# Last tap of v's convolution: ScalarE and an accumulating transfer in place of a VectorE operation

## The reference, cut to what matters

```python
q = _silu(x @ Wq); k = _silu(x @ Wk); v = _silu(x @ Wv); z = x @ Wz
q = _causal_dwconv(q, conv_q_w)      # depthwise, 4 taps: y[t] = sum_i w[i] * u[t - 3 + i]
k = _causal_dwconv(k, conv_k_w)
v = _causal_dwconv(v, conv_v_w)
...                                  # rotary embedding and normalization of q and k
for s in range(4):
    k_s, v_s, a_s = _lag(k, s), _lag(v, s), _lag(a, s)
    attn = einsum('bshd,bshd->bsh', q, k_s) * scale
    out = out + (attn * sigmoid(a_s * b))[..., None] * v_s
out = out * rsqrt(mean(out * out) + eps) * norm_w * _silu(z)
return out @ Wout
```

## Time and profile before

| | us |
|---|---|
| median of 3 runs | 1383.82 |
| fastest and slowest run | 1382.62, 1384.70 |
| profiled execution | 1383.09 |
| its span, first to last instruction | 1381.0 |
| TensorE busy | 1350.4 |
| VectorE busy | 988.1 |
| ScalarE busy | 737.9 |
| GpSimd busy | 333.3 |

### The profile page before, as it was taken

How to read it: one execution, slowest core, us unless ns; L and a number is a source line. 1 busy time by engine, 2 the same in 40 slices (tenths; PEclk the granted TensorE clock), 3 DMA queues, 4 the chain that set the end, 5 groups by cost and what they waited for, 6 DMA issues and landing times. The chain is left out here.

```text
span 1381.0 us, 23144 instructions
## 1 busy us (share of the span) xinstructions
PE 1350.4 (98%) x6824; PEld 1140.7 (83%) x6824; DVE 988.1 (72%) x1529; ACT 737.9 (53%) x2209; POOL 333.3 (24%) x508
## 2 busy tenths in 40 slices
PE   6999999999999999999999999996999999999998
PEld 4788888888888888888888888885888888888886
DVE  7898998989999999999998999983122222234443
ACT  5656665656656666666566665652654434432221
POOL 6134242323333232323333332422000000000001
PEclk9999999999999999999999999997999999999999
DMA  8233434334344344343433434333421101156454
GB/s 287 62 87 86 101 78 115 93 85 97 95 93 100 85 104 102 80 100 83 108 93 85 100 85 108 78 75 74 152 96 50 46 23 47 36 186 188 129 174 157
DMA packets 123418, 138.79 MB, mean 101 GB/s; under 512 B 30704, under 2 KB 67568, under 8 KB 123120
## 3 DMA queue, kind: packets, MB, share of 16 engines
q1 hardware_dynamic: 114160, 121.48, 31.1%
q0 software_dynamic: 9216, 16.78, 7.1%
HBM read 62.58 MB, written 25.30 MB: 64 GB/s over the span
## 5 line engine op out<-in xcount | busy, mean ns | idle before, releaser
L1169 DVE TENSOR_TENSOR hid_lo<-relu,hid_hi 128x512 fp32r<-128x512 f32 x64 | 44.3, 693 | 172.8 <-ACT hid_hi L1115 172.8
L670 DVE SCALAR_TENSOR_TENSOR y_v<-u_v,cw_v,y_v 128x512 f32<-128x512 f32 x192 | 144.8, 754 | 29.0 <-ACT y_v L561 24.3
L670 DVE SCALAR_TENSOR_TENSOR y_k<-u_k,cw_k,y_k 128x512 f32<-128x512 f32 x192 | 145.2, 756 | 26.1 <-ACT y_k L561 19.2
L581 ACT ACTIVATE bank<-bank 128x128 f32<-128x128 f32 x512 | 133.8, 261 | 46.7 <-PE bank L866 46.4
L670 DVE SCALAR_TENSOR_TENSOR y_q<-u_q,cw_q,y_q 128x512 f32<-128x512 f32 x192 | 144.1, 750 | 19.4 <-ACT y_q L561 10.5
L472 POOL TENSOR_TENSOR rq_win<-rq_win,const 128x32 f32<-128x32 f32 x64 | 21.4, 335 | 478.4 <-DMA rq_win<-rq_scratch 478.4
L1210 DVE TENSOR_TENSOR hid_lo<-o_raw,hid_hi 128x512 fp32r<-128x512 f32 x64 | 44.3, 692 | 101.4 <-ACT hid_hi L1135 101.4
L459 POOL TENSOR_TENSOR rnorm<-norms,neg_half 128x8 f32<-128x8 f32 x64 | 108.4, 1693 | 9.9 <-POOL norms L455 8.9
L1111 ACT ACTIVATE relu<-bank,us_sb 128x512 f32<-128x512 f32 x64 | 44.1, 689 | 121.9 <-PE bank L1250 121.9
L1135 ACT ACTIVATE hid_hi<-o_raw 128x512 fp32r<-128x512 f32 x64 | 40.4, 632 | 121.9 <-PE bank L1280 119.2
L1087 POOL TENSOR_TENSOR g_buf<-g_buf,up_raw 128x512 f32<-128x512 f32 x3 | 3.8, 1281 | 403.2 <-DVE g_buf L1190 403.2
(11 more groups left out here) (170 smaller groups left out, 3455.5 us busy)
## 6 DMA issues: line engine op xcount, KB each, us to landing
swapped_q<-y_q SPq DMA_DIRECT2D x128, 128.0 KB, 2.3
swapped_k<-y_k SPq DMA_DIRECT2D x128, 128.0 KB, 2.3
sq_sum<-out_sq POOLq DMA_DIRECT2D x64, 256.0 KB, 3.3
o_scratch<-o_buf SPq DMA_DIRECT2D x64, 256.0 KB, 2.6
o_raw<-o_scratch SPq DMA_DIRECT2D x64, 256.0 KB, 3.2
raw_q<-in_wq SPq DMA_DIRECT2D x16, 256.0 KB, 3.1
raw_k<-in_wk SPq DMA_DIRECT2D x16, 256.0 KB, 3.5
raw_v<-in_wv SPq DMA_DIRECT2D x16, 256.0 KB, 4.4
```

The source lines that it names most:

```text
L581: last = nc.scalar.activation(block_of, block_of, ACT.Square, accum_out=norms[:, g1 % 2, i * BC + b:i * BC + b + 1])
L670: nc.vector.scalar_tensor_tensor(y[n][:, g % 2, :], u[n][:, g % 2, i:i + CH], cw[n][:, bass.ds(h * TAPS + i, 1)], y[n][:, g % 2, :], ALU.m ...
L1169: nc.vector.tensor_tensor(hid_lo[:, j % 2, :], relu[:, j % 2, :], hid_hi[:, j % 2, :].bitcast(fp32), ALU.subtract).then_inc(hid_lo_done, 1)
```

## The change

The last tap of v (i = 3) is no longer an operation of VectorE. ScalarE makes the product as a scaled copy of `u["v"]` into a buffer of its own, `last_tap`, right behind the first tap. GpSimd's queue adds it to `y["v"]` by an accumulating DMA of 256 KB. GpSimd issues it at the beginning of the next step, ahead of the norms, once ScalarE's copy and VectorE's two remaining taps are done. `turn_v` waits for the landing of this DMA in place of VectorE's third tap. `last_tap` takes the place of `down_raw[:, 1]`, so the second group of FFN weights is loaded in the FFN part and no longer in the prologue.

```diff
+        DVE_TAPS = {"q": 3, "k": 3, "v": 2}
         sq_asked = sem("sq_asked", ctx)
+        last_tap_made = sem("last_tap_made", ctx)
+        last_tap_asked = sem("last_tap_asked", ctx)
+        last_tap_added = sem("last_tap_added", ctx)
+        last_tap = down_raw[:, 1, :, :]
...
-            for i in range(2):
-                env["load_ffn_weights"](sp, i)
+            env["load_ffn_weights"](sp, 0)
             sp.wait_ge(cleared, 6)
...
+            def add_last_tap(g1, c):
+                wait(pool, last_tap_made, c)
+                wait(pool, conv_done["v"], 2 * c)
+                pool.sem_inc(last_tap_asked, 1)
+                nc.gpsimd.dma_start(y["v"][:, g1 % 2, :], last_tap[:, g1 % 2, :], accum_op=ALU.add
+                                    ).then_inc(last_tap_added, 16)
+
             def step(h, g):
                 c = h * G + g
+                if back(h, g, 1):
+                    add_last_tap(back(h, g, 1)[1], c)
                 if at := back(h, g, 1):
...
                 if n == "v":
+                    wait(act, last_tap_added, 16 * (c - 1))
                     wait(act, turned_v, c - 1)
...
+                if n == "v":
+                    nc.scalar.activation(last_tap[:, g % 2, :], u["v"][:, g % 2, HALO:], ACT.Copy,
+                                         scale=cw["v"][:, bass.ds(h * TAPS + HALO, 1)]
+                                         ).then_inc(last_tap_made, 1)
...
                     conv_tap("v", 2, h, g, c)
-                    conv_tap("v", 3, h, g, c)
...
             def turn_v(g1, c):
                 wait(pe, norms_done, c)
-                wait(pe, conv_done["v"], 3 * c)
+                wait(pe, last_tap_added, 16 * c)
...
-            for i in range(2, FT // WG):
+            for i in range(1, FT // WG):
                 wait(sp, up_signed, i - 1)
                 wait(sp, down_signed, i - 1)
                 load_ffn_weights(sp, i)
```

More of the change, by code:

```diff
@@ L544, in silu_and_tap @@
                 wait(act, proj_done[n], c + 1)
-                wait(act, conv_done[n], 3 * (c - 1))
+                wait(act, conv_done[n], DVE_TAPS[n] * (c - 1))
                 nc.scalar.activation(u[n][:, g % 2, HALO:], bank[:, :], ACT.Silu).then_inc(silu_done[n], 1)
-                wait(act, conv_done[n], 3 * c)
+                wait(act, conv_done[n], DVE_TAPS[n] * c)
                 wait(act, silu_done[n], 2 * c + 1)
                 if n == "v":
+                    wait(act, last_tap_added, 16 * (c - 1))
                     wait(act, turned_v, c - 1)
@@ L668, in conv_tap @@
                 else:
-                    wait(dve, conv_done[n], 3 * c + i - 1)
+                    wait(dve, conv_done[n], DVE_TAPS[n] * c + i - 1)
                 nc.vector.scalar_tensor_tensor(
```

## The result

The changed kernel takes 1416.44 us (median of 4 runs, 1414.1 to 1418.87) where the kernel before took 1384.26 beside it. The ratio is 1.0234, with an interval of 1.0214 to 1.0255. That is 32 us slower; the forecast was 26, and its range went up to 1428 us. The profiled execution took 1417.08 us, its span 1415.3 against 1381.0 before.

A forecast was written before the change was run, and what follows sets the result against it. The prediction took attention to be bound by TensorE. Steady steps 14, first late step 2.5, start 5.4, clock 2.5 and end 1.7 summed to 26.1 us on 1383.1, giving 1409 us; own range 1402 to 1422, 8-in-10 range 1393 to 1428.

The forecast's parts named there:

- VectorE and ScalarE cost and give nothing: Attention: 49 us taken from VectorE gain 0; ScalarE's added 0.72 us copy a step costs 0, at most 11 us.
- The need of a steady step: Steady attention steps: time needed from sq_sum's issue to `turn_v`, between 4.5 and 5.8 us, taken as 5.6.
- On average half of d is paid: Steady steps: `turn_v` late by d (0.4 typically, mean 0.8 at g=1) pays half on average, 14 us over 56 steps.
- rival 1: Steady steps hide the transfer, need 4.5 to 5.0; 11 to 14 us lost, 1396 us; chance 0.30.
- How often a g = 1 step is late: Second step of a head: room before `turn_v` 5.0 us in 8 of 13 heads, 4.4 in 5.
- The start: Second `turn_v`: its transfer stands behind `gate_k`, which waits for VectorE's gates; 5.4 us of stall (4.7 to 6.3).
- The clock's 2.0 for 2.5: Behind the start's stall: TensorE's clock may fall to half speed, costing 2.5 us (0 to 3.8).
- The first late step: Head 1, still unrolled: sq_sum only 2.17 us ahead of `turn_v`; 2.5 us of stall (1.6 to 3.4).
- The end: End of attention: last `turn_v` 3.3 to 3.9 us late, half absorbed by a later idle; 1.7 us (0.5 to 2.5).
- SP's loads: Second group of FFN weights moved from prologue to FFN's start: hidden by about 2 us, cost 0.
- Rival 2: Steady steps: second accumulating transfer starts its 3.3 us only once the first has landed; need 6.8, 1446 us; chance 0.12.
- Rival 3: Attention: VectorE did bound, so up to 49 us come back, less the start's 8; down to 1342 us; chance 0.05.

The follow-up runs named there:

- experiment 1: The kernel before without v's last tap on VectorE and nothing in its place: 1383.75 us, ratio 0.9997.
- experiment 2: The kernel before with ScalarE's copy and GpSimd's transfer added, into a buffer nobody reads, VectorE's tap kept: 1382.16 us, ratio 0.9985.
- experiment 5: The changed kernel with an operation of the tap's size on VectorE where the tap was, on data nobody reads: 1418.68 us, ratio 1.0251.
- experiment 4: The changed kernel with `gate_k` of chunk 0 moved behind the last tap's transfer of chunk 1: 1405.58 us, ratio 1.0171.
- experiment 9: The kernel before with only the second group of FFN weights moved to the FFN's start: 1383.94 us, ratio 0.9998.
- experiment 8: The changed kernel with VectorE's two products with sin written as scalar_tensor_tensor by 1.0: 1415.31 us, ratio 1.0235.

## Why the prediction was right, and where its sizes were off

**VectorE and ScalarE cost and give nothing.** Right (experiments 1 and 2). The 0.77 us back to SP in g = 1 steps are nearly right too: against the kernel before the two kinds of room grow by 0.71 and 0.74, and between experiment 5 and the changed kernel by 0.64 to 0.68.

**The need of a steady step.** Its two ends were 4.5 and 5.8, and the value taken, 5.6, is right for a step in which the store overlaps: 5.66. The way there was not quite the forecast's: the second issue begins 0.69 us after the first, not 0.95, and the landing takes 4.9, not 4.65 (5.6 less 0.95). The hint of the rows that the DMA engines are full held: in line behind sq_sum the landing is 4.2 (0.8 more than alone), and with the store 4.9 (0.7 more). By the figures of the Trainium skill (DMA: Bandwidth & Descriptors, Anatomy of one DMA) a landing after 2.6 us is the estimate for 256 KB. The traces disagree: no accumulating transfer of this queue in any run landed in under 3.3.

**The failed step: "On average half of d is paid", with d = 0.4 in a typical step.** The forecast took one need, 5.6, for all steps, because it let the store's bytes start 0.8 us after their issue, in the middle of the new ones. In a typical step with g = 2 or 3 they don't: sq_sum comes 5.2 us ahead, the store is issued 2.6 later and its first packet starts only at 4.33, the need is 5.0, and the stall is zero, as in rival 1. In a late step sq_sum comes about 0.6 later, the store (which VectorE times) now meets the new bytes, and the need jumps to 5.66. Room falls by 0.6 and the need rises by 0.7 at once. The stall is then 1.0 to 1.3 (2.4 once), and paid in full: the step before has no stall that would give it room, and the step behind has no d of its own to be relieved of. So the sum is 15 stalls (12.6 + 6.6), 2.0 of shorter delays and 1.7 of clock, 22.9, where 56 times 0.25 gave 14.

By kind of step, the miss is in g = 1: half of a mean d of 0.8 gave 5.6 us, and 12.9 were paid (a mean of 0.92). The other 42 steps were put at half of 0.4, 8.4 us, and lost 8.4 without the clock. That agreement is luck, for it came from five g = 3 stalls and some short delays and not from all steps alike.

**How often a g = 1 step is late.** The forecast's two kinds were right: rooms of 5.0 and 4.4 were to be had, and the better ones had 4.97, the stalled ones 4.39. But it took the late kind in 5 of 13 heads, as before, and it came in 9 of 13 (and step 61 stalls as well). VectorE's last tap moved forward by 0.71 us and the window operation by 0.49, so more of them miss the tap's end. The trace of the kernel before shows the edge to whoever lines the window operation up with VectorE's taps, though not on which side each step would fall.

**The start.** 5.1 for 5.4, and experiment 4 confirms the order on GpSimd as its cause. The clock's 2.0 for 2.5 is right in kind: the clock fell within the idle, and the first 4.2 us of work behind it (to 76.8) ran at half of it.

**The first late step (2.5).** It cost 0.02 at step 5. The stall at the start had shifted TensorE by 7.5 us, but GpSimd's chain less, so sq_sum was 5.37 ahead of `turn_v` and not 2.17. The forecast had stated this very rule (a stall leaves the chain in place) and not carried it from the start to here. 1.6 us came at step 6 instead, so the start in all was 9.4 for 10.4.

**The end.** 1.8 for 1.7. The last `turn_v` idles 3.58 us (forecast 3.3 to 3.9), and the tail takes 1.9 of the 3.7 back:

```profile
973.66 0.63 PE L856 MATMUL bank<-const,y_v 128*128 128x128 f32 x4 [3.58 <-DMA y_v<-down_raw]
```

**SP's loads.** 0, right (experiment 9).

**The rivals.** Rival 1 (steady steps hide it) is the typical step but not the whole. Rival 2 (one transfer after the other) falls by its sign: in a typical step the second transfer has landed 4.9 us behind the first issue (0.69 + 4.2), 1.5 behind the first landing, and not 6.6. Rival 3 (VectorE bounds) falls by experiment 1. The direction and the places of the loss were understood; that the total came within 6 us is in part luck, because an average stood in for two kinds of step. Its 14 us should have had a further range upward.

## What to carry to other kernels

A transfer that takes the place of an operation has to be costed from its issue to its landing, in the place in the queue that it gets, and with what another queue sends meanwhile; here 3.4 us alone became 4.2 in second place and 4.9 beside a store. When one engine's small operation ends with another's long one, ask on which side of it the operation will fall once the other engine runs earlier: an edge of a few hundredths of a microsecond was worth 0.6 here. Ask of a queue's program what the new entry stands behind (GpSimd's wait for VectorE's gates had cost nothing, and now cost 5.1 and the clock 2.0), and issue first what the bound engine waits for: the order alone was worth 22 of 23 us in the steady steps. When the engine that binds is busy for 98%, relief of another engine buys nothing, and a small margin should be costed step by step and not by its mean, since one delay can both take room and raise the need.

## What the runs showed of the hardware

- Two accumulating transfers of GpSimd's queue of 256 KB each overlap: in the changed kernel's typical step the second lands 1.5 us after the first, not 3.4.
- SP's store of 256 KB has its first packet 0.86 us after its issue when nothing else is in flight, and 1.70 after it in step 15, where it waits out nearly all of the second accumulating transfer. Issued 0.6 us earlier (step 13) it gets in between, and that transfer lands 0.7 later.
- GpSimd's issue of the second begins 0.69 us after that of the first, though each row shows 0.94 or more; the rows of issues overlap.
- A GpSimd operation of 128x32 elements takes 0.24 us, or up to 0.81 when it ends 0.10 us behind an operation of VectorE that was running beside it. The edge lies 0.11 to 0.12 us before the end of VectorE's operation. Its mean went from 0.34 to 0.62 us by taking an operation away from VectorE (experiment 1).
- A stall can cost more through the clock. TensorE's stayed at 2.4 GHz over the idle of 1.80 us in experiment 4 and over those of 1.81 in experiment 5 (step 17 for one). It fell to 1.2 in the idle of 4.93 and just behind that of 2.25. It isn't the length of the last idle alone: before the last `turn_v` of experiment 8 TensorE idles 2.48, and the granted clock stays at 1.00 there:

```profile
970.31 0.63 PE L856 MATMUL bank<-const,y_v 128*128 128x128 f32 x4 [2.48 <-DMA y_v<-down_raw]
```
```profile
970.00:972.00 2.00, 1.69 (x10) 1.51 (x11) 0.00 (x0) 0.60 (x1) 0.22 (x1) 1.00 0.20 38
```
